# Attention stage of a graph transformer: VectorE's scaling before its statistics, the output norm three to four steps later, and GpSimd's gathers and roots in another order

## The reference

```python
X = heads(lrelu(nodes @ W_lin + b_lin)); q = heads(lrelu(nodes @ W_q)); k = heads(lrelu(nodes @ W_k))
att = sigmoid(einsum('bhxd,bhyd->bhxy', q, k) * scale)
adj_h = adj_matrix[:, None] * att
deg = sum(adj_h, axis=-1)
dis = where(deg > 0, deg ** (-0.5), 0.0)
Y = einsum('bhxy,bhyd->bhxd', dis[..., :, None] * adj_h * dis[..., None, :], X)
x = x + (Y - mean(Y)) * rsqrt(var(Y) + 1e-5) * ln_g + ln_b
```

## Time and profile before

| | |
|---|---|
| median of 3 runs | 1538.24 us (1538.18 to 1538.66) |
| the profiled execution's own time | 1539.02 us |
| its span (first to last instruction) | 1537.3 us |
| busy in the span | PE 1401.7 us (91%), DVE 1021.2 (66%), ACT 748.2 (49%), POOL 720.7 (47%) |
| attention stage, sigmoid of its first step to end of its last | 668.4 to 1183.3 us |
| mean granted TensorE clock | 0.984 |

### The profile page before, as it was taken

One profiled execution on the slowest core, in us unless ns is written; L12 is line 12 of the kernel. 1 busy time (PEld: TensorE's weight loads), 2 busy tenths in 40 slices (PEclk: granted clock), 3 DMA queues, 4 the chain that ended last, 5 costly groups with the idle time before them and its releaser, 6 DMA issues. The chain is left out here.

```text
span 1537.3 us, 25067 instructions
## 1 busy us (share of the span) xinstructions
PE 1401.7 (91%) x9010; PEld 808.8 (53%) x9010; DVE 1021.2 (66%) x2212; ACT 748.2 (49%) x1184; POOL 720.7 (47%) x500
## 2 busy tenths in 40 slices
PE   4999999899999999977899988998999779999998
PEld 2455545669999998732222222222222357773488
DVE  2467767633333333368788999999987789967732
ACT  3365565534444444446454554655554457872110
POOL 1127776740000000749787887876233479981000
PEclk9999999999999999999999999999999999999999
DMA  9757637276788775633342424423322231004024
GB/s 300 254 188 282 235 118 228 88 205 203 229 230 231 233 228 159 171 118 125 96 129 90 124 84 122 142 84 119 91 90 69 69 95 42 15 1 90 1 85 138
DMA packets 207599, 215.26 MB, mean 140 GB/s; under 512 B 23269, under 2 KB 164709, under 8 KB 207476
## 3 DMA queue, kind: packets, MB, share of 16 engines
q1 hardware_dynamic: 199284, 196.81, 41.9%
q0 software_dynamic: 8192, 16.86, 3.5%
HBM read 168.54 MB, written 45.07 MB: 139 GB/s over the span
## 5 line engine op out<-in xcount | busy, mean ns | idle before, releaser
L1417 ACT ACTIVATE c_AH<-c_S 128x2048 f32<-128x2048 f32 x128 | 240.6, 1879 | 235.5 <-PE c_S L1314 235.5
L1447 DVE TENSOR_TENSOR c_AH<-c_AH,c_A 128x2048 f32<-128x2048 f32 x128 | 313.0, 2454 | 44.2 <-ACT c_AH L1417 43.9
L1242 POOL DMA_INDIRECT G<-ys,slots x102 | 195.4, 1915 | 32.7 <-issue 28.0
L810 ACT ACTIVATE a_A<-a_DG,a_A 128x256 f32<-128x256 f32 (+1 forms) x192 | 93.8, 527 | 208.3 <-PE a_DG L677 207.0
L530 POOL DMA_INDIRECT rows<-a_S,a_slots x128 | 134.0, 1047 | 49.9 <-issue 38.1
L557 POOL DMA_INDIRECT a_A<-ys,slots x16 | 16.4, 1024 | 292.9 <-DMA ys<-a_A 288.3
L1341 PE MATMUL c_DG<-c_AH,c_ones 128*32 128x512 f32 x1024 | 138.1, 612 | 12.0 <-DVE c_AH L1447 12.0
L1327 PE MATMUL c_YA<-c_AH,c_XT 128*32 128x512 f32 x1024 | 137.9, 620 | 12.1 <-DVE c_XT L1500 12.1
L1314 PE MATMUL c_S<-c_Q,c_K 32*128 32x512 f32 x928 | 135.2, 653 | 14.5 <-DVE c_K L1532 7.8
L648 PE MATMUL a_AG<-a_A,x 128*128 128x512 f32 x256 | 114.1, 599 | 5.1 <-DVE a_Z L891 5.1
L677 PE MATMUL a_DG<-a_A 128*128 128x256 f32 (+1 forms) x336 | 99.9, 420 | 7.1 <-ACT a_A L810 6.0
(11 more groups left out here) (393 smaller groups left out, 2566.2 us busy)
## 6 DMA issues: line engine op xcount, KB each, us to landing
a_A<-in_dram SPq DMA_DIRECT2D x72, 578.0 KB, 4.0
a_A<-in_dram SPq DMA_DIRECT2D x32, 1024.0 KB, 10.0
c_A<-in_dram SPq DMA_DIRECT2D x128, 256.0 KB, 2.8
a_A<-rows SPq DMA_DIRECT2D x71, 129.0 KB, 3.3
ys<-a_A SPq DMA_DIRECT2D x71, 128.0 KB, 2.3
a_X<-in_dram SPq DMA_DIRECT2D x8, 512.0 KB, 13.0
a_R<-in_dram SPq DMA_DIRECT2D x8, 512.0 KB, 5.3
stream<-a_R SPq DMA_DIRECT2D x8, 512.0 KB, 10.0
```

Of the source, the lines that this page charges most:

```text
L810: act.activation(hT[g % 2][:, f, 0:size(g)], up_bank(g, f)[:, 0:size(g)], ACT.Gelu, bias=w_of(g)[:, F_N + f:F_N + f + 1]).then_inc(h_ready, 1)
L1242: pool.indirect_dma_start(Gt[k][:, t, :], None, ys, bass.IndirectOffsetOnAxis(ap=slots[:, k, T * i + t:T * i + t + 1], axis=0), bounds_che ...
L1417: act.activation(AH[g % UNITS][:, :, :], S[:, :, :], ACT.Sigmoid, scale=HD ** -0.5).then_inc(att_ready, 1)
L1447: dve.tensor_tensor(ah[:, :, :], ah[:, :, :], A[g % ADJ_BUFS][:, :].unsqueeze(1).to_broadcast([P, HEADS, HALF]), ALU.mult).then_inc(ah_dve, 1)
```

## The change

It moves instructions within three lists; none is added or removed. For graphs 0 and 1 `stats_x` goes to steps 3 and 4 and `apply_x` to 5 and 6. On DVE, `scale_X(i - 1, 1)` stands ahead of `stats_x` where both fall in step 4 (graph 1), and `leak_qk(K, .., "k1")` ahead of the multiply of step 1. `stats_y` moves from step 5 to 8, `gain_Y` from 8 to 10 and 11 in halves of four, `finish` from 9 to 13. On POOL, four of the last eight gathers of a graph stand ahead of `norm_y.power`, and the last four stand behind `root(i, 0)`, directly ahead of `combine`; for graph 2 the first two gathers stand ahead of the first `norm_in.power`.

```diff
-STATS_AT = (4, 4)
+STATS_AT = (3, 4)
...
             combine(1)
+            gather(2, range(2))
             norm_in.power(pool, power, 0, 0)
-            gather(2, range(10))
+            gather(2, range(2, 10))
...
+                gather(i + 2, range(8, 12))
+                if is_graph(i - 2) and i - 2 < B - 1:
                     norm_y.power(pool, power, i - 2, i % 2)
...
-                gather(i + 2, range(8, 16))
                 if is_graph(i):
                     root(i, 0)
+                gather(i + 2, range(12, 16))
                 if is_graph(i + 2):
                     combine(i + 2)
...
-            def gain_Y(i):
-                for t in range(T):
+            def gain_Y(i, half):
+                for t in range(4 * half, 4 * half + 4):
...
-                dve.wait_ge(yg_ready, i + 1)
+                dve.wait_ge(yg_ready, NH * i + NH)
...
+                    if n == 1 and is_graph(i):
+                        leak_qk(K, i, "k1")
                     if is_graph(i):
                         multiply(STEPS * i + n)
+                    if n == 4 and is_graph(i - 1):
+                        scale_X(i - 1, 1)
                     if n == stats_step(i) and i < B:
                         stats_x(i + 1)
-                    if n == 1 and is_graph(i):
-                        leak_qk(K, i, "k1")
...
-                    if n == 4 and is_graph(i - 1):
-                        scale_X(i - 1, 1)
-                    if n == (6 if i < len(STATS_AT) else 4) and is_graph(i + 1):
+                    if n == (stats_step(i) + 2 if i < len(STATS_AT) else 4) and is_graph(i + 1):
                         apply_x(i + 1)
...
-                    if n == 5 and is_graph(i - 2) and i - 2 < B - 1:
+                    if n == 8 and is_graph(i - 2) and i - 2 < B - 1:
                         stats_y(i - 2)
-                    if n == 8 and is_graph(i - 2) and i - 2 < B - 1:
-                        gain_Y(i - 2)
-                    if n == 9 and is_graph(i - 2) and i - 2 < B - 1:
+                    if n in (10, 11) and is_graph(i - 2) and i - 2 < B - 1:
+                        gain_Y(i - 2, n - 10)
+                    if n == 13 and is_graph(i - 2) and i - 2 < B - 1:
                         finish(i - 2)
```

## The result

The changed kernel takes 1518.39 us in the median of 4 runs (1517.11 to 1521.11), the one before, on the same chip, 1538.21 (1537.93 to 1538.66): ratio 0.9873, 95% interval 0.9856 to 0.9890, 19.8 us less. The profiled execution took 1519.38 us, its span is 1517.7 us, where before it was 1537.3.

The account below looks back on a forecast made before the run. The prediction held that waits between the closely matched lists of PE, DVE and POOL bound the attention stage. Terms -4.8, -15.2, -2.4 and 0 gave -22.4 us, from 1539.0 to 1516.6, forecast 1516 us; range 1502 to 1531.

Parts of the forecast that it names:

- the forecast case: Whole kernel: DVE's and POOL's lists both near 62 to 63.5 us a graph, total 1508 to 1523 us; chance 0.57.
- DVE's idle 4.79 us: Graph 1: DVE's gap while PE waits for XT goes once scaling precedes the statistics; taken as -4.8 us.
- the lower bound, 6.9: Graph 1: best bound of -6.9 us, if the clock loss and the K wait of that graph go as well.
- the landing wait: POOL, graphs 2 to 5: the combine waits for its last gathers to land, taken as 2.9 us.
- 62.8 by DVE's list: Graphs 2 to 5: DVE's busy 61.9 us plus 0.9 for steps 1 to 4 limit each graph, giving -15.2 us.
- POOL would run without slack: Graphs 2 to 5: POOL's cycle of 59.5 us plus 2.9 is 62.4, just below the 62.8 us a graph.
- costed at nothing: POOL's new order, graphs 2 to 5: no cost beyond the 62.8 us, roots reaching DVE's step 4 about when wanted.
- the shift does not fall on a multiply of step 5: Graphs 6 and 7: the reason why step 8 loses little there; -0.6 us taken for graph 6.
- PE as the bound: Rival 1, graphs 1 to 7: PE's list sets 59.3 us a graph, -42 us at most, 1504 in the middle; chance 0.13.
- POOL late: Rival 2, graphs 3 to 5: late landing or roots give 64.5 to 65.5 us each, total 1526; chance 0.17.
- Rival 4: Steps 8 and 13: the moved DVE statistics and finish stop PE as long as before, total 1536 to 1541; chance 0.05.
- The rule that was weighed: Skill's inference that DVE's tensor_tensor does not hold up gathers' descriptor generation; the sum went by a row of 2.83 us instead.

Follow-up runs that it names:

- e5: The changed kernel with POOL's residual shift of graphs 2 to 5 behind the third group of four gathers: 1514.50 us, ratio 0.9821 to the kernel before.
- e3: The kernel before with only POOL's new order of gathers and roots in the steady graphs: 1564.31 us against 1570.84, ratio 0.9975.
- u_output: The changed kernel with output statistics, norm weights and finish back at steps 5, 8 and 9: 1529.19 us, ratio 0.9895 to the kernel before.
- u_pool: The changed kernel with POOL's old steady order, eight gathers between the root for Y and that of the degrees: 1534.99 us, ratio 0.9943 to the kernel before.
- e2: The kernel before with only DVE's output statistics, norm weights and finish moved to steps 8, 10 and 11, and 13: 1565.33 us against 1570.84, ratio 0.9968.
- x_shift_last: The changed kernel with the residual shift of graphs 6 and 7 behind their root for Y: 1513.13 us, ratio 0.9820 to the kernel before.
- x_both: The changed kernel with the residual shift moved behind the third gathers (graphs 2 to 5) and the root for Y (6, 7): 1541.47 us against 1569.69 before, ratio 0.9826.
- e6: The changed kernel with the last four gathers ahead of the root of the degrees again: 1543.20 us against 1541.14 for the kernel before, ratio 1.0010.
- e4: The kernel before with graph 1's input statistics and apply one step earlier, two gathers ahead of POOL's first root: 1569.34 us against 1570.84, ratio 1.0011.
- u_scale: The changed kernel with the scaling of X back behind the statistics in step 4 of graph 1: 1523.43 us, ratio 0.9869 to the kernel before.

## Why the prediction was right, and where it was not

**The forecast, 1516 us, was 2.4 us low.** The measured time lies in the forecast case. That it is so near is in part luck: graph 1 gained 2.5 us more than forecast and graph 7 1.2 more, graph 6 lost 3.9 against its forecast, and the start of the stage and graph 0 differ for reasons outside the change. By its own terms:

| term | forecast | measured |
|---|---|---|
| graph 0 | 0 (-1 to +2) | -1.4, within the spread of repetitions |
| graph 1 | -4.8 (0 to -6.9) | -7.3 |
| graphs 2 to 5 | -15.2, 62.8 us each | -14.8, 62.9 each |
| graph 6 | -0.6 | +3.3 |
| graph 7 | -1.8 | -3.0 |
| start of the stage | not in the sum | +3.4 |

*Graph 1* was mis-sized. The forecast took DVE's idle 4.79 us. What shrank is the period of the stop itself, 10.96 to 4.20 us (-6.8), with a clock loss behind it (5.02 to 4.16, -0.9) and the leak of K at the end (5.10 to 3.22, -1.9). Three periods grew by 2.2 us together (0.9, 1.0 and 0.3, steps 8 to 10). So the wait of about 1 us came (1.07 for `XT`, timeline of PE), DVE has no gap, and the lower bound, 6.9, was the nearer value.

*Graphs 2 to 5* came out right in the sum, but only in part by the forecast's items. Right: step 8 at 5.2 us (its period gave 14.9 us in the four graphs), the wait for the bank read gone, the landing wait at 2.1 us in the mean where 2.9 was taken. Left out: the leak of K, no longer behind POOL's sum, returned 1.9 us in graphs 3 and 4 (0.6 and 4.3 in 2 and 5); and the sum came to fall on step 15 and the scaling there, which cost 1.5 us at step 4 (2.6 in graph 2) and some 0.3 ahead of it. These two nearly cancel. "62.8 by DVE's list" was thus a fair price for the place where the three lists meet, not a proof that DVE's list is the limit: e5 reached 61.6 with the same list.

*"POOL would run without slack"* was wrong. The forecast wanted hardly any wait for the statistics of Y; POOL waits for them up to 6.0 us a graph, 21.8 us in four. Its gathers take 1.59 us in the mean of these graphs (65 of them, by POOL's groups); their mean over all 102 is 1.64 to 1.73 us in every run with POOL's new order (e3 and u_output too) and 1.83 to 1.92 in every run with the old one, so they are shorter with that order. POOL's cycle without waits is about 62.9 - 21.8 / 4 - 2.1 = 55.4 us, where the forecast had 59.5.

*POOL's order "costed at nothing"* is the step whose reason was thinnest. Undoing it costs 19.0 us (u_pool), the most of all parts, and undoing the later output norm 12.0. Without POOL's order the later norm only moves the stop from step 8 to steps 2 and 3, with the root late by 3.9 us (e2, u_pool). What either gives by itself is not settled: a loss of 1.2 and 0.2 us by the sums of e2 and e3, a gain of 5.5 and 6.5 by their medians. The prediction looked at what the order does to `x_ready`; what decides is the root of the degrees, for which DVE waits, and where the sum falls.

*Graph 6* is the step that failed, outside its own bounds (0 to a gain): "the shift does not fall on a multiply of step 5" holds, but the shift fell on the multiply of step 4, made `XT` late by 2.52 us, and behind that wait PE's granted clock fell to 0.57 over 4 us: 65.3 us instead of 61.4. x_shift_last shows it by moving that one instruction (62.1). *Graph 7* gained 3.0 at three places: 5.09 to 4.20 at step 6, 4.79 to 4.15 at step 8, and 6.50 to 4.99 at step 12, the only one that the forecast had named.

*The rivals.* PE as the bound was not reached: 62.7 us against its 59.3; x_both comes to 61.6 in graphs 3 to 5. POOL late is seen in the experiments that leave its order as it was, not in the change. Rival 4 is nearest to what e2 alone does: the stop moves, from step 8 to steps 2 and 3.

*The rule that was weighed.* The gathers that start inside a multiply end late, as the earlier trace rows had it: in the changed kernel one that starts at 905.09, 0.3 us behind a multiply, takes 2.84 us, one beside `apply_x` at 936.03 takes 1.02. So the inference in the Trainium skill (SBUF — State Buffer, section Who interferes with whom), that a tensor_tensor of DVE leaves descriptor generation alone, is not borne out here either. Its rule on GpSimd instructions that read SBUF agrees with every stretched pair above.

*Still open:* how much of the gain in graphs 2 to 5 the earlier leak of K in step 1 has, since it wasn't tried alone; what the kernel before takes in this stage from run to run, and with it what each part gives alone; and whether an order exists in which the sum falls into an idle stretch of DVE in every graph.

## What to carry to other kernels

When work moves on one engine, follow its result through the in-order list of the engine that consumes it: whatever is queued behind that consumer is moved too, and the edit pays only with the order over there changed as well. Two engines that block each other lose about the same wherever they meet (mostly 2.0 to 2.4 us here), so ask on which instruction the meeting falls and who waits for that one. Parts of such a change can't be priced one at a time and added: undone one by one, three of them cost 19.0, 12.0 and 5.5 us, together 36.5, where the whole change gives 21.8. And profile the version you start from more than once: a single one can't tell an edit of a few us from how its engines happened to meet.

## What the runs showed of the hardware that was not expected

- An add of 128x1024 on POOL made DVE instructions with two operands in SBUF wait, however small they were: the 128x16 product took 2.35 us instead of 0.17, the leak of K 2.82 instead of 0.68, a chain of eight small ones (`finish`) 6.44 instead of 2.18, with two adds beside it. The stop is about the same 2 us for each add, so its share of a small instruction is enormous.
- A gather that starts inside a multiply mostly ends 0.9 us behind the end of that multiply: 905.09 + 2.84 = 907.93 with the multiply (904.75 + 2.29) done at 907.04. It can take longer: in e6 one that started at 924.44, just behind the start of a multiply, took 5.98 us, through that multiply, the leak of K and the next multiply, and ended 0.9 us behind the second one, which ended at 929.51.
- POOL's root of 16 values in each partition takes 2.90 to 7.17 us over all runs, as long as an add of 128x1024 (2.3 to 4.5) or longer; short lists of such roots are no small change in POOL's cycle.
- How two engines stand to each other, once set, carries over from graph to graph: in e4 the last step of graphs 2 to 5 takes 7.27, 7.70, 8.09 and 8.22 us, and graphs 3 and 4 last 2.7 and 2.9 us longer than before. Whether the edit of e4 set it or the run would have had it anyway is not shown.
- The same wait of PE can leave its clock up or bring it down: behind 2.52 us for `XT` in graph 6 the granted clock was 0.57 over 4 us in the changed kernel and 1.00 in u_scale, a difference of 1.6 us.
